# Attention output of jobs 4 to 14 kept feature-major: transfers in place of transposes, on one Trainium2 core

## The reference

```python
attn = jnp.einsum('blhd,bmhd->bhlm', q, k) * scale
attn = jax.nn.softmax(attn, axis=-1)
out = jnp.einsum('bhlm,bmhd->blhd', attn, v).reshape(B, L, D)
return out @ Wproj + bproj
```

## Time and profile before

| | us |
|---|---|
| median of 3 runs | 1045.67 (1043.49 to 1047.11) |
| the profiled execution | 1044.84 |
| its span, first to last instruction | 1042.0 |
| TensorE busy | 1020.8 (98%) |
| VectorE busy | 694.8 (67%) |
| ScalarE busy | 797.9 (77%) |
| GpSimd busy | 492.0 (47%) |
| DMA engines, mean share | 23% |

### The profile page before, as it was taken

How to read it: one execution, slowest core, us unless ns; L and a number is a source line. 1 busy time by engine, 2 the same in 40 slices (tenths; PEclk the granted TensorE clock), 3 DMA queues, 4 the chain that set the end, 5 groups by cost and what they waited for, 6 DMA issues and landing times.

```text
span 1042.0 us, 19622 instructions
## 1 busy us (share of the span) xinstructions
PE 1020.8 (98%) x6697; PEld 672.6 (65%) x6697; DVE 694.8 (67%) x1416; ACT 797.9 (77%) x1332; POOL 492.0 (47%) x446
## 2 busy tenths in 40 slices
PE   7999999999999999999999999999999999999995
PEld 5888898856757656666566666666666566545442
DVE  6755348573473672447857866966857866999984
ACT  3574656599898798887787887888877877786783
POOL 2563844706446255535337437345354356247051
PEclk9999999999999999999999999999999999999998
DMA  7010000422404213122042222212302121232220
GB/s 260 1 52 10 2 21 21 113 78 56 129 11 113 52 42 103 32 82 62 2 102 85 81 57 72 64 30 73 82 12 62 33 72 48 54 100 53 71 58 25
DMA packets 36384, 64.43 MB, mean 62 GB/s; under 512 B 7208, under 2 KB 22312, under 8 KB 36288
## 3 DMA queue, kind: packets, MB, share of 16 engines
q1 hardware_dynamic: 36288, 63.20, 22.8%
HBM read 22.90 MB, written 2.12 MB: 24 GB/s over the span
## 4 chain that ended last, share of the span: by engine, by line
PE 85%; issue 6%; POOL 4%; DVE 3%; ACT 1%; DMA 0%; SPq 0%; DVEq 0%; POOLq 0%; ACTq 0%
PE rings L548 15%; PE AVB L660 15%; PE rings L550 13%; PE rings L549 13%; PE rings L647 10%; PE rings L622 7%; PE rings L591 2%; PE rings L695 2%; PE rings L700 2%; PE rings L572 1%; POOL gT_l L1280 1%; PE rings L712 1%; PE rings L630 1%; DVE m L1174 1%; PE rings L675 1%
## 5 line engine op out<-in xcount | busy, mean ns | idle before, releaser
L854 ACT ACTIVATE probs<-rings 128x512 f32<-128x512 f32 x568 | 301.3, 611 | 83.0 <-PE rings L647 51.0
L1177 DVE TENSOR_REDUCE m<-rings 128x1 fp32r<-128x512 f32 x386 | 244.0, 682 | 51.9 <-PE rings L622 44.7
L660 PE MATMUL AVB<-probs,V 128*32 128x512 f32 x1536 | 200.9, 602 | 1.0 <-issue 1.0
L647 PE MATMUL rings<-SQ,SK 64*128 64x512 f32 x768 | 177.2, 436 | 1.0 <-DMA SQ<-cT 0.7
L1280 POOL TENSOR_TENSOR gT_l<-gT_f,gT_h 128x512 fp32r<-128x512 f32 x96 | 121.8, 1295 | 112.7 <-ACT gT_h L914 111.6
L647 PEld LDWEIGHTS rings<-SQ,SK 64*128 64x128 f32 x768 | 82.4, 185 | 91.4 <-issue 38.5
L622 PE MATMUL rings<-SK,SQ 63*128 63x512 f32 x512 | 130.3, 435 | 0.0
L548 PE MATMUL rings<-w_h,gT_h 128*128 128x256 f32 x384 | 111.4, 290 | 0.0
L851 ACT ACTIVATE probs<-rings 128x1024 f32<-128x1024 f32 x100 | 98.8, 1043 | 12.4 <-issue 8.9
L549 PE MATMUL rings<-w_l,gT_h 128*128 128x256 f32 x384 | 106.7, 278 | 0.0
L550 PE MATMUL rings<-w_h,gT_l 128*128 128x256 f32 x384 | 106.6, 278 | 0.0
(11 more groups left out here) (191 smaller groups left out, 2128.5 us busy)
## 6 DMA issues: line engine op xcount, KB each, us to landing
SQ<-qh SPq DMA_DIRECT2D x96, 128.0 KB, 2.6
SK<-kh SPq DMA_DIRECT2D x96, 128.0 KB, 2.7
SQ<-ql SPq DMA_DIRECT2D x48, 128.0 KB, 2.7
SK<-kl SPq DMA_DIRECT2D x48, 128.0 KB, 2.9
raw<-in_w SPq DMA_DIRECT2D x20, 256.0 KB, 2.8
wmod_s<-in_wmod SPq DMA_DIRECT2D x6, 512.0 KB, 4.1
gates<-gate_rows SPq DMA_DIRECT2D x12, 256.0 KB, 3.7
raw<-in_wqkv SPq DMA_DIRECT2D x9, 256.0 KB, 2.7
```

The costliest lines, as they stand in the source:

```text
L647: mm = pe.matmul(o[:, :], SK[a % 4][r:r + KS + 1, n // 2, c * P:(c + 1) * P], SQ[a % 4][r:r + KS + 1, n // 2, :], start=True, stop=True)
L660: mm = pe.matmul(AVB[32 * n:32 * n + 32, :], V[j % 2][:, i, (HD + 1) * h:(HD + 1) * h + 32], probs[:, (4 * t + n) % PROBS, :], start=(i == ...
L854: act.activation(probs[:, n % PROBS, :], bank(kind, a, i)[:, :], ACT.Exp, scale=SCALE[layer(unit_job(a))]).then_inc(done["scores"], 1)
L1177: nc.vector.tensor_reduce(m16[:, col:col + 1], bank(kind, a, i)[:, :], AX_X, ALU.max, negate=True).then_inc(done["max"], 1)
```

## The change

In jobs 4 to 14 the steps `o` and `O` are gone; job 15 keeps them. In their place stand `x` (take), `j` (sums), `l` (divide) and `J` (oN). The columns of V are laid out anew, a head's features two columns apart and the constant in the 16th of its 32 columns, so that in AVB and `oU` a head's features stand in every second of its 32 rows and its sum in row 15. For each unit one DMA packs its 64 feature rows into half of `oc` (the memory of `tok2`), and one DMA copies its 4 rows of sums 16 times each into half of `rc` (the memory of `tmp`). For each half of the features VectorE takes the reciprocal of all 128x512 sums and multiplies. ScalarE and VectorE then write `postT_h` and `postT_l` from `oc` as they did from PSUM. The order in TURNS is a new one throughout. The core of the diff:

```diff
-              "gatecast": (many, 1), "oT1": (many, TT), "oT2": (many, CH), "hT2": (ffn, CH), "fc1": (ffn, MT),
+              "gatecast": (many, 1), "oT1": (jobs[-1:], TT), "oT2": (jobs[-1:], CH),
+              "take": (moved, UNITS), "sums": (moved, UNITS), "divide": (moved, CH), "oN": (moved, CH), "hT2": (ffn, CH), "fc1": (ffn, MT),
...
+    "s a wd a2 lf s6 Q l j a x C Z s2 l s2 Q C J s X J Z s K s2 Q wf Q Z v Z R p2 I N s2 lf s3 a3 s2 C s2 r B N2 s7 "
+    "s5 a2 x2 s3 j2 Q j l s4 j x a l Z a J X s6 Q2 Z Q Z J a Z R a p2 I s4 N s2 lq B N K N2 lq r s5 a2 M s7 a C a q "
+    "s4 d h2 s2 a2 s7 j2 x l j2 a J s a2 s l s4 c J k s4 a p2 s6 K a s2 wq B M b s2 a2 s6 a q2 k H2 v2 lg s4 f4 C "
+    "s m2 a s2 m2 s m a x m s t j2 s3 h m4 a2 s2 t m2 s m h m s4 l j2 y l s4 J2 q k q p2 m3 s3 a2 t m t s3 m2 a s Y "
+    "s m2 j2 a s3 m3 x a m s2 m s m s m s2 m s m s l h2 m2 x m2 ld a3 j s l s J2 t lr wd K t s m q k p2 m s m2 s m "
+    "s a s m s m h2 m4 a2 m s m s2 m a l j x s l s3 J2 t2 q v k p s2 m s m2 p s2 m4 q s4 a2 B m s3 m2 a m3 M s3 k K "
+    "s m3 j s a X m s2 j3 s a t x t s m2 s3 l a m s5 l a2 m J2 s m3 s lq q p2 m2 s m a m s3 k s m s X s t wq B q k "
+    "s3 m2 a m2 s3 m2 K a m j3 V m3 l j q x s4 a l J k lg s4 t2 a2 J s2 m3 q p s4 m2 p m s3 m2 a m3 B m v k s4 m2 "
...
+        VW = HEADS * (HD + 2)
+        V = [sb(f"V{i}", [P, TT, VW]) for i in range(2)]
+        oc = tok2[:, :, :].rearrange("p (c t) d -> p c (t d)", c=CH)
+        rc = tmp[:, :, :].rearrange("p (c t) d -> p c (t d)", c=CH)
...
+                elif kind == "take":
+                    sp.wait_ge(unit_out, UNITS * (a - BATCH) + i + 1)
...
+                    r = 64 * (i % 2)
+                    sp.dma_start(oc[r:r + 64, i // 2, :], oU[0:P:2, i, :]).then_inc(taken[i], 16)
+                elif kind == "sums":
+                    sp.wait_ge(unit_out, UNITS * (a - BATCH) + i + 1)
...
+                    s = oU[HD - 1:HD, i, :]
+                    src = bass.AP(s.tensor, s.offset, [[32 * UNITS * TOK, 4], [0, HD], [1, TOK]])
+                    sp.dma_start(rc[r:r + 64, i // 2, :], src).then_inc(summed[i], 16)
...
-                    pe.wait_ge(done["oT2"], nth("oT2", a, 0 if a < JOBS - 1 else i))
+                    pe.wait_ge(*post_ready(a, 0 if a < JOBS - 1 else i))
...
-                    if g == 0 and j > BATCH:
-                        act.wait_ge(pe_ring, use("oT1", j - 1, TT - 1))
+                    if j > BATCH:
+                        act.wait_ge(taken[g], MOVED_IN(j - 1))
+                        act.wait_ge(summed[g], MOVED_IN(j - 1))
...
+                elif kind == "oN":
+                    act.wait_ge(done["divide"], nth("divide", a, i))
+                    if i == 0:
+                        act.wait_ge(pe_ring, use(*POST_READ[(kind, a, i)]))
+                    act.activation(postT_h[:, i, :], oc[:, i, :], ACT.Identity,
+                                   bias=colv[:, layer(a), C_V + i:C_V + i + 1]).then_inc(hi_in[kind], 1)
...
+                elif kind == "divide":
+                    for g in (2 * i, 2 * i + 1):
+                        dve.wait_ge(summed[g], MOVED_IN(a))
+                    link(nc.vector.reciprocal(rc[:, i, :], rc[:, i, :]))
+                    for g in (2 * i, 2 * i + 1):
+                        dve.wait_ge(taken[g], MOVED_IN(a))
+                    nc.vector.tensor_tensor(oc[:, i, :], oc[:, i, :], rc[:, i, :], ALU.mult).then_inc(done[kind], 1)
+                elif kind == "oN":
+                    dve.wait_ge(hi_in[kind], nth(kind, a, i))
+                    nc.vector.scalar_tensor_tensor(out=postT_l[:, i, :], in0=oc[:, i, :],
+                                                   scalar=colv[:, layer(a), C_V + i:C_V + i + 1],
+                                                   in1=postT_h[:, i, :].bitcast(F32), op0=ALU.add, op1=ALU.subtract
+                                                   ).then_inc(done[kind], 1)
```

More of the change, by code:

```diff
@@ L219 @@
 for _s in PLAN:
-    if _s[0] in ("hT2", "oT2") and _s[2] == 0:
+    if _s[0] in ("hT2", "oT2", "oN") and _s[2] == 0:
         POST_READ[_s] = _reader
@@ L296, in cond_blocks_kernel @@
         SK = [sb(f"SK{i}", [P, 2, TOK], F32R) for i in range(4)]
-        VW = HEADS * (HD + 1)
-        V = [sb(f"V{i}", [P, TT, VW + 16]) for i in range(2)]
+        VW = HEADS * (HD + 2)
+        V = [sb(f"V{i}", [P, TT, VW]) for i in range(2)]
         probs = sb("probs", [P, PROBS, TOK])
@@ L335, in bank @@
             return ring[USE[(kind, a, i)] % RING]
-        kinds = sorted({s[0] for s in PLAN if not s[0].startswith("load") and s[0] not in ("stack", "crow", "store", "gelu", "gateout", "gatecast", "gatefix", "fold")})
+        kinds = sorted({s[0] for s in PLAN if not s[0].startswith("load") and s[0] not in ("stack", "crow", "store", "gelu", "gateout", "gatecast", "gatefix", "fold", "take", "sums")})
         done = {k: sem("done_" + k) for k in kinds}
@@ L345, in cond_blocks_kernel @@
         sq_ready = sem("sq_ready")
-        hi_in = {k: sem("hi_" + k) for k in ("hT1", "hT2", "oT2")}
+        hi_in = {k: sem("hi_" + k) for k in ("hT1", "hT2", "oT2", "oN")}
         w_hi = sem("w_hi")
@@ L374, in cond_blocks_kernel @@
         final_dve = sem("final_dve")
+        taken = [sem(f"taken{g}") for g in range(UNITS)]
+        summed = [sem(f"summed{g}") for g in range(UNITS)]
         first_in = [sem(f"first_in{n}") for n in range(8)]
@@ L381, in STACK_IN, with MOVED_IN @@
             return 16 * 6 * ((u - UNITS * BATCH) // 4 + 1)
+        def MOVED_IN(j):
+            return 16 * (j - BATCH + 1)
         def GATE_IN(j):
@@ L543, in claim, with post_ready @@
                 return ring[n % RING]
+            def post_ready(a, n):
+                kind = "oN" if a < JOBS - 1 else "oT2"
+                return done[kind], nth(kind, a, n)
             def product(out, stationary, moving, first, last):
@@ L659, in _ @@
                         h = 4 * g + n
-                        mm = pe.matmul(AVB[32 * n:32 * n + 32, :], V[j % 2][:, i, (HD + 1) * h:(HD + 1) * h + 32],
+                        r = 2 * (HD + 1) * (h % 8) + (HD + 1) * (h // 8)
+                        mm = pe.matmul(AVB[32 * n:32 * n + 32, :], V[j % 2][:, i, r:r + 32],
                                        probs[:, (4 * t + n) % PROBS, :],
@@ L719, in _ @@
                             if c > 0 and a < JOBS - 1:
-                                pe.wait_ge(done["oT2"], nth("oT2", a, c))
+                                pe.wait_ge(*post_ready(a, c))
                             src = [h[:, c, tok:tok + P] for h in (postT_h, postT_l)]
@@ L1006, in _ @@
                         dve.wait_ge(pe_av, nth("av", UNITS * (a - 1) - 1, TT - 1))
-                        sums = V[a % 2][:, :, 0:VW].rearrange("p t (h e) -> p t h e", e=HD + 1)[:, :, :, HD:HD + 1]
-                        nc.vector.memset(sums, DIM ** 0.5).then_inc(done[kind], 1)
+                        for first in (2 * HD, HD - 1):
+                            ins = nc.vector.memset(V[a % 2][:, :, first:first + 7 * (2 * HD + 2) + 1:2 * HD + 2], DIM ** 0.5)
+                        ins.then_inc(done[kind], 1)
                 elif kind == "gate":
@@ L1042, in _ @@
                     dve.wait_ge(hi_in[kind], nth(kind, a, i))
-                    if a == JOBS - 1:
-                        tok = slice(DIM * i, DIM * (i + 1))
-                        for c in range(CH):
-                            ins = nc.vector.scalar_tensor_tensor(out=postT_l[:, c, tok], in0=bank(kind, a, i)[:, DIM * c:DIM * (c + 1)],
-                                                                 scalar=colv[:, layer(a), C_V + c:C_V + c + 1],
-                                                                 in1=postT_h[:, c, tok].bitcast(F32),
-                                                                 op0=ALU.add, op1=ALU.subtract)
-                    else:
-                        ins = nc.vector.scalar_tensor_tensor(out=postT_l[:, i, :], in0=bank(kind, a, i)[:, :],
-                                                             scalar=colv[:, layer(a), C_V + i:C_V + i + 1],
-                                                             in1=postT_h[:, i, :].bitcast(F32), op0=ALU.add, op1=ALU.subtract)
@@ L1054, in _ @@
-                    ins.then_inc(done[kind], 1)
+                    tok = slice(DIM * i, DIM * (i + 1))
+                    for c in range(CH):
+                        ins = nc.vector.scalar_tensor_tensor(out=postT_l[:, c, tok], in0=bank(kind, a, i)[:, DIM * c:DIM * (c + 1)],
+                                                             scalar=colv[:, layer(a), C_V + c:C_V + c + 1],
+                                                             in1=postT_h[:, c, tok].bitcast(F32),
+                                                             op0=ALU.add, op1=ALU.subtract)
@@ L1067, in _ @@
                     if multi(a):
-                        dve.wait_ge(pe_ring, use("oT2", a, CH - 1))
+                        dve.wait_ge(done["oN"], nth("oN", a, CH - 1))
```

49 lines of the change are left out of this document (24 added, 25 removed), and 75 rows, old and new, of tables (CODE, TURNS).

## The result

The changed kernel takes 1148.3 us (median of 4 runs, 1143.5 to 1149.2) against 1044.6 of the kernel before on the same chip: ratio 1.098, 95% interval 1.094 to 1.101. I forecast 1069 and a range from 1036 to 1092: the direction was right, the size wrong by 79 us.

What follows compares the result with a forecast made beforehand. TensorE (98% busy, 85% of the chain) was taken to bind, with VectorE also binding from 868 to 1016 us. 868.0 - 16.5 + 31.4 + 157.5 + 26.0 + 2.8 gave 1069 us, 2.2% slower; range 1036 to 1092.

Steps and rivals of the forecast that it cites:

- Edits that I price at nothing. The DMAs: 88 transfers of 128 KB, each landing in 2.6 us, covered by the first divide; without cover up to +11 us.
- Where it lies beside other work: Jobs 4 to 11: TensorE waits at the projection for VectorE's divides in seven jobs, 31.4 us with contention.
- the end stretch: From job 13's first score tile to the tail: VectorE's 148.9 us plus 8.6 us of waits, 157.5 against 148.
- What goes from TensorE: The transposes of oT1 and oT2 in 11 jobs, 2.69 us a job, 29.6 us together.
- rival 4: Transposes were covered by other waits, so the change moves nothing: 1045 us; chance 0.04.
- Rival 1: VectorE's halves are hidden in jobs 4 to 11 and only the end binds: 1038 us, 0.7% faster; chance 0.20.
- 3 (a cheap reciprocal): Reciprocal costs a plain pass, 0.69 us, so TensorE's 29.6 us are all gained: 1015 us; chance 0.06.
- Rival 2: GpSimd holds each of 40 VectorE instructions outside job 6 for 1.1 us, not 0.32, +31: 1100 us; chance 0.08.

Runs made afterwards that it cites:

- e12: Changed kernel with e4's order, without the 88 transfers, a plain pass in place of the reciprocal (no division, no packing): 1031.0 us, ratio 0.987.
- e11: e4 without its 88 transfers; the divide step takes the reciprocal of a constant once its half is copied: 1090.0 us, ratio 1.044.
- e4: Changed kernel with the sums landing in postT's low half, each issued right behind its unit's take: 1122.0 us, ratio 1.074.
- e5: e4 with a plain pass in place of the reciprocal, so it divides by no sum: 1085.8 us, ratio 1.040.
- e2: Changed kernel with a plain VectorE pass over the same tile in place of the reciprocal; transfers and waits stay: 1115.3 us, ratio 1.067.
- e18: e14 with the transfers issued from ScalarE's queue, each pair behind the copy of its unit: 1075.1 us, ratio 1.029.
- e14: e12 with the 88 transfers back, issued by SP with e4's waits, into DRAM that nothing reads: 1071.9 us, ratio 1.026.
- e13: Kernel before, with a 3.35 us reciprocal of a constant ahead of each of the 22 oT2 evictions on VectorE: 1134.4 us, ratio 1.085.
- e15: Kernel before with e13's 22 reciprocals, both of a job placed behind its second oT2 eviction: 1129.5 us, ratio 1.082.
- e6: Kernel before with one of four transposes in each oT1 and oT2 of jobs 4 to 14: 1038.9 us, ratio 0.995.
- e7: e4 with proj, stat2, norm2 and hT2 some 6 us of TensorE work further back in the order: 1227.1 us, ratio 1.174.
- e9: e4 in the order of work of the kernel before, each SP transfer directly behind the step it waits for: 1177.9 us, ratio 1.127.
- e16: e5 with each step of SP's queue directly behind the step that it waits for: 1096.2 us, ratio 1.049.

## Why the prediction was wrong in size

The runs from e12 to the changed kernel make a sum, and TensorE's busy and idle time (parts 1 of the pages; idle is span less busy) shows what each step adds:

| kernel | median | span | PE busy | PE idle | clock |
|---|---|---|---|---|---|
| before | 1044.6 | 1042.0 | 1020.8 | 21.2 | 0.997 |
| e12: no transposes, no transfers, no reciprocals | 1031.0 | 1031.3 | 1006.9 | 24.4 | 0.993 |
| e11: + reciprocals | 1090.0 | 1090.1 | 1035.4 | 54.7 | 0.969 |
| e4: + transfers, early | 1122.0 | 1117.8 | 1037.8 | 80.0 | 0.968 |
| after: + sums late | 1148.3 | 1145.6 | 1048.9 | 96.7 | 0.948 |

By step that is -14, +59, +32 and +26. That they add up to the 104 is no proof, since each row starts from the one above. The price of a part depends on what else is there: from e12 over e5 and e2 to the changed kernel the early transfers come first, at 55, then their late issue at 30 and the reciprocals at 33. So the transfers cost 58 to 84 us and the reciprocals 33 to 59.

From e12 to after the span grows by 114.3 us: TensorE is idle for 72.3 us more and busy for 42.0 us more with the same 6433 matmuls. Set side by side matmul by matmul, 37.9 of the 42.0 us fall on the 296 that start at 1.2 GHz. Busy time alone does not say so: in e18 it is 22 us above e12 at full clock.

**The step that failed** is "Edits that I price at nothing. The DMAs". I let the landing of one transfer (2.6 us) stand for eight a job: from the last copy of oU to the landing I had 4.4 us, had "the first `l` (4.04)" cover it "but for some tenths", and gave "+11" as the upper bound. In job 9 the same stretch took 11.7 us, from the copy at 688.70 to the second reciprocal, which starts at 700.43 when the last sums are in. The transfers cost 58 to 84 us in all, in three ways. The sums go out late, because `tmp` is taken and stacks stand ahead of them (26, e4). SP's queue is held, and the stacks and shifts with it, which I had put at 0 to 0.6 us a job (41 us with nobody reading, e14). And a `sums` is not a `qh`. Its semaphore is updated five times, once at the issue and four times at the landing, where that of a `take` is updated 16 times: it runs on four DMA engines. The first of a row lands 4.3 to 4.7 us after its issue; in job 9 the next ones follow 2.7 to 3.0 us apart, while SP's issue stretches to 2.5 us. The Trainium skill, "DMA: Bandwidth & Descriptors", under "Why a DMA increments its semaphore by 16 and not by 1", says that the number of engines is the largest, up to 16, that divides the size of the outermost dimension on both sides. The source here has four rows outermost, which gives four, and the trace agrees. I had not held that against the new access pattern.

**"Where it lies beside other work"** and the end stretch priced VectorE's new work at 31.4 + 9.5 = 41 us; the reciprocals are worth 33 in the changed kernel (e2), 36 with early sums (e4 against e5) and 59 without transfers (e11 against e12). So the size was fair, and that the direction came out was not luck; but the place was wrong. I let TensorE wait for VectorE only at the first `p`: it stood there 19.9 us for my 31.4, and 38.1 us at score tiles and tiles for the maximum, for VectorE, ScalarE and the shift rows, where I had nothing. e13 and e15 show that the reciprocals stop TensorE ahead of `p` as well as behind it: in e15 eleven holds of 6.7 us add 53.0 us of idle time and 31.4 us of busy time with the same matmuls, 4.8 and 2.9 us each, and 29.4 of the 31.4 fall on matmuls that start at 1.2 GHz. This second part, the clock, is in no term of my sum.

**"What goes from TensorE"** was sized by its rows, and I credited 16.5 us of the 29.6 in the sum; 14 came back in the new order, and 5 of 22 in the old one (e6). Here the size was near, but rival 4 had more in it than the 0.04 that I gave it: back-to-back matmuls did not make their removal worth their time, and "TensorE's work in steps is therefore time", read from its 98%, does not hold in e6.

**What held:** the reciprocal, 3351 ns for my 3.35; VectorE's total, 750 for 755; the weight load's wait, 28.2 for some 30. (Its row names `postT_l` for 4.9 us of that and nothing for 19.0; in the trace 22.5 us end less than 0.1 us behind an `oN` on VectorE.) Not so: the first score tile of job 13, at 947.6 and not 883; the stretch behind it, 172 us for 157.5, with VectorE busy for 85% and not over 93%. In job 6, which I gave nothing, VectorE stood 10.2 us for its sums.

The count of 8 that the Trainium skill gives for a reciprocal ("VectorE: DVE Perf Modes", "First, the fixed hardware budget") would have made it an estimated 4.3 us; 512 columns in 3351 ns are 6.3 cycles of its 0.96 GHz each, and the measurement decides.

**The rivals.** Rival 1 (hidden) and 3 (a cheap reciprocal) are gone. Rival 2 named contention with GpSimd, and my sum had 1.3 us a job for it. The products took 692 ns and `oN` 747, and no single one was held. But this doesn't refute it: in the trace 42 of the 44 ran while GpSimd had no instruction, and the other two had started first. The `qknorm` row from which I took the 1.1 us has all five of its long ones (1155 to 1779 ns) beside a running instruction of GpSimd. So it was a matter of when they ran, which I had not looked at. The last sentence of the prediction, that waits for shifts or DMAs would show SP's queue mis-priced, came true in part: TensorE's own waits for shift rows are 7.5 us here, and e14 shows what else hangs on them.

Open: why e6 gives back so little of its 22 us; whether SP's waits or its issues hold the shift rows; and whether an order made for the measured times in all five queues could win back more than e4 did. That was tried only by the simple moves of e7, e9 and e16, and each made it worse.

## What to carry to other kernels

An engine that is idle for a third of the time can still be without room: in a kernel whose queues run in order, price a long instruction by what stands behind it until the next engine runs dry, plus the slower clock that came behind the wait (in e15 6.7 us of VectorE cost 7.7 us). A transfer put between two engines costs its issue, what its wait holds in the issuing queue, and the number of engines that its access pattern allows, not the landing time of another transfer of the same size. Before trading work away from the fullest engine, leave that work out in a run: 22 us of it were worth 5.

## What was not expected of the hardware

- The granted clock fell to the lower level during or just behind TensorE's waits of 1.3 to 9.3 us and stayed there for 3.4 to 13.7 us, 120 us in all; matmuls of 256 columns spanned 0.41 in place of 0.28 us.
- A 128 KB transfer that copies four rows to 64 partitions landed in 4.3 to 5.1 us alone or as the first of a row and in 9.4 as the fourth of one (job 9); one of the same size between 64 partitions on either side had a median of 3.3.
- Issuing such a transfer took SP 0.62 us in the median and up to 2.5 us when others issued just ahead were still under way; on ScalarE's queue (e18), where each followed a single `take`, it took 0.56 us in the median.
- Two-input passes in SBUF ran at 692 to 747 ns on average in a kernel where GpSimd is busy for 43%, and none was held; 42 of the 44 met no instruction of GpSimd.
